# A decoder layer on one core: GpSimd overwrites the small router logits, and every engine's order is laid out anew

## The reference, cut to what matters

```python
x = _layernorm(x + _L0_attn_ref(x, ...))     # gated recurrence, 16-head attention, gated feed-forward
x = _layernorm(x + _L0_xattn_ref(x, ctx, ctx, mask, ...))   # attention over a context
x = _layernorm(x + _L0_ffn_ref(x, Wr, Wi, Wo))              # 8 experts, 2 chosen per token
```

```python
probs = jax.nn.softmax(xf @ Wr, axis=-1)      # 8 router logits per token
topk_p, topk_i = jax.lax.top_k(probs, 2)
# output: the sum over the two chosen experts of topk_p * (xf @ Wi[e] @ Wo[e])
```

## Time and profile before

| | us |
|---|---|
| median of 3 runs | 226.48 (226.40 to 226.54) |
| profiled execution | 226.43 |
| its span, first to last instruction | 224.5 |
| PE busy | 207.8 |
| DVE busy | 183.7 |
| ACT busy | 172.1 |
| POOL busy | 140.3 |

### The profile page before, as it was taken

The page is one execution under the profiler, slowest core; times in us unless marked ns, Lnnn a source line. Parts: engine busy times, 40 slices in busy tenths (PEclk is TensorE's granted clock), DMA queues, the critical chain, the costliest instruction groups (busy, mean ns, idle before and its releaser), DMA issues.

```text
span 224.5 us, 6962 instructions
## 1 busy us (share of the span) xinstructions
PE 207.8 (93%) x2170; PEld 173.5 (77%) x2170; DVE 183.7 (82%) x667; ACT 172.1 (77%) x663; POOL 140.3 (62%) x302
## 2 busy tenths in 40 slices
PE   7889999999999999999999999999989999998840
PEld 3568988999988799799778988798786899884310
DVE  3573775579879789988998999989988897999984
ACT  4799988987798796889699889986668867646730
POOL 5464535637568775777468766975648847547452
PEclk9999999999999999999999999999999999999997
DMA  4988745555742324002400555445460000000001
GB/s 99 252 256 191 181 110 134 149 149 137 172 107 52 105 55 108 0 7 49 108 1 4 123 140 127 109 116 102 127 154 13 5 25 15 16 0 1 12 23 35
DMA packets 33716, 20.05 MB, mean 89 GB/s; under 512 B 20497, under 2 KB 31249, under 8 KB 33681
## 3 DMA queue, kind: packets, MB, share of 16 engines
q1 hardware_dynamic: 32992, 19.35, 34.2%
q10 hardware_dynamic: 688, 0.26, 0.4%
HBM read 14.16 MB, written 5.24 MB: 86 GB/s over the span
## 4 chain that ended last, share of the span: by engine, by line
PE 49%; DVE 14%; DMA 9%; SPq 8%; issue 7%; ACT 7%; POOL 5%; POOLq 0%; DVEq 0%; ACTq 0%
PE ps L966 8%; DMA k_stack<-qk_scratch 5%; PE ps L931 5%; PE ps L843 4%; PE ps L1048 4%; SPq L276 4%; PE ps L898 4%; PE ps L920 4%; PE ps L989 4%; DMA ctx_sb<-in_ctx_dram 3%; PE ps L900 2%; PE ps L877 2%; PE ps L857 2%; DVE acc L2488 2%; ACT probs L1707 2%
## 5 line engine op out<-in xcount | busy, mean ns | idle before, releaser
L2373 DVE TENSOR_REDUCE neg_max<-ps 128x4 f32<-128x512 f32 x64 | 43.1, 677 | 4.7 <-PE ps L900 4.4
L1707 ACT ACTIVATE probs<-ps 128x512 f32<-128x512 f32 x64 | 38.4, 606 | 4.8 <-PE ps L920 4.5
L464 POOL TENSOR_TENSOR lrs<-mv,neghalf 128x1 f32<-128x1 f32 x48 | 26.5, 553 | 24.0 <-DVE mv L2418 8.4
L464 POOL TENSOR_TENSOR rs<-ss,neghalf 128x1 f32<-128x1 f32 x48 | 27.1, 567 | 20.7 <-ACT junk L1626 20.5
L966 PE MATMUL ps<-xT,guT 128*128 128x128 f32 x256 | 34.0, 276 | 0.0
L1048 PE MATMUL ps<-w_moe,y2T 128*128 128x512 f32 x64 | 32.6, 599 | 0.4 <-ACT terms L1786 0.4
L966 PEld LDWEIGHTS ps<-xT,guT 128*128 128x128 f32 x256 | 31.2, 192 | 0.3
L524 POOL TENSOR_SCALAR_AFFINE_SELECT probs<-probs 128x600 f32<-128x600 f32 x32 | 24.2, 758 | 8.1 <-ACT probs L1707 7.8
L898 PE MATMUL ps<-k_stack,q_stack 125*128 125x128 bf16 x256 | 24.9, 219 | 1.3 <-DMA k_stack<-qk_scratch 1.3
L920 PE MATMUL ps<-q_stack,k_stack 128*128 128x128 bf16 x256 | 24.8, 219 | 0.0
L920 PEld LDWEIGHTS ps<-q_stack,k_stack 128*128 128x128 bf16 x256 | 18.8, 99 | 3.8 <-issue 2.3
(11 more groups left out here) (156 smaller groups left out, 584.9 us busy)
## 6 DMA issues: line engine op xcount, KB each, us to landing
q_stack<-qk_scratch SPq DMA_DIRECT2D x48, 96.0 KB
k_stack<-qk_scratch SPq DMA_DIRECT2D x48, 96.0 KB
qk_scratch<-qk_parts SPq DMA_DIRECT2D x16, 192.0 KB, 2.2
ctx_sb<-in_ctx_dram SPq DMA_DIRECT2D x4, 256.0 KB, 3.5
qk_scratch<-qk_parts SPq DMA_DIRECT2D x16, 64.0 KB, 2.4
out_dram<-x_all SPq DMA_DIRECT2D x16, 64.0 KB, 1.6
x_all<-in_x_dram SPq DMA_DIRECT2D x2, 256.0 KB, 3.1
raw<-in_L_ffn_Wi_dram SPq DMA_DIRECT2D x1, 512.0 KB, 6.0
```

The lines of the kernel that those rows point to most:

```text
L464: nc.gpsimd.tensor_tensor(dst, src, neghalf[:], ALU.pow).then_inc(S[rsd], 1)
L1707: nc.scalar.activation(probs[:, b, n, :, :], view("probs", 4 * k + n), ACT.Exp, scale=HD ** -0.5).then_inc(S["att_p"], 1)
L2373: nc.vector.tensor_reduce(neg_max[:, b, QUARTER * n:QUARTER * n + QUARTER], view("scores", 4 * k + n), AX_X, ALU.max, negate=True).then_in ...
```

## The change: what it does

The overwriting of the six columns moves from DVE to POOL, as a step `moe_pad` of its own between `moe_top` and `moe_choose`; `moe_choose` waits for it:

```diff
+            def moe_pad(k):
+                b = k % 2
+                after(pool, "moe_top", k + 1)
+                nc.gpsimd.memset(top[:, b, CHOSEN:EXPERTS], NO_LOGIT).then_inc(S["moe_pad"], 1)
...
             def moe_choose(k):
                 b = k % 2
-                nc.vector.memset(top[:, b, CHOSEN:EXPERTS], NO_LOGIT).then_inc(S["moe_pick"], 1)
-                after(dve, "moe_pick", 3 * k + 1)
+                after(dve, "moe_pad", k + 1)
                 nc.vector.match_replace(moe_new[:, b, :], top[:, b, :], moe_lg[:, b, :], -NO_LOGIT).then_inc(S["moe_pick"], 1)
-                after(dve, "moe_pick", 3 * k + 2)
+                after(dve, "moe_pick", 2 * k + 1)
```

Waits that the new orders imply are left out, and waits that they need are put in:

```diff
-            def power(src, dst, ready, k, rsd, used):
+            def power(src, dst, ready, k, rsd):
-                after_all(pool, (ready, k + 1), (used, k - 1))
+                after(pool, ready, k + 1)
...
             def ffn_residual(k):
-                after(pool, "ffn_z", k - 1)
...
             def moe_add(k):
-                after(pool, "moe_high", k - 1)
...
             def att_values(k):
-                after(pe, "max_v", k + 1)
...
             def ffn_hidden(k, fill, g, done):
+                after(pe, "ffn_xT", k + 1)
...
             def gru_squares(k):
+                after_all(act, ("gru_rs", k - 1))
...
             def gru_tanh(k):
+                after(act, "gru_xs", k - 1)
+                after(act, "gru_decay", k - 1)
...
             def ctx_copy(k):
-                after(act, "ctx_kv_ps", k - 1)
```

More of the change, by code:

```diff
@@ L49 @@
[L49 to L62, removed]
@@ L372, in _ @@
             parts_stack(4)
+            parts_save(5)
             load_ctx(3)
-            parts_save(5)
             load_small()
@@ L377, in _ @@
             parts_stack(5)
+            parts_save(6)
             load_x(3)
-            parts_save(6)
             max_stack(4)
@@ L389, in _ @@
             max_stack(8)
+            store(0)
             parts_save(9)
             parts_stack(9)
+            store(1)
+            max_stack(9)
             parts_save(10)
-            max_stack(9)
             parts_stack(10)
-            store(0)
             parts_save(11)
-            store(1)
             store(2)
@@ L411, in _ @@
             parts_save(15)
-            store(5)
             max_stack(13)
@@ L416, in _ @@
             max_stack(15)
+            store(5)
             store(6)
@@ L757, in _ @@
             xat_ln_power(14)
+            moe_pad(13)
+            moe_pad(14)
             moe_ln_power(11)
@@ L762, in _ @@
             moe_ln_power(12)
+            moe_pad(15)
             moe_ln_power(13)
@@ L1324, in _ @@
             ffn_gate(6)
-            moe_experts(3, 0)
+            ffn_up(6)
             moe_logits(4)
@@ L2719, in _ @@
             moe_top(3)
[L2720 to L2741 removed]
+            moe_moments(2)
+            moe_choose(3)
+            moe_weights(3)
+            gru_scan(10)
+            ffn_silu(6)
+            ffn_product(6)
+            moe_layernorm(1)
+            xat_add_mask(5)
+            moe_top(4)
+            ffn_out(6)
+            moe_choose(4)
+            ffn_stats(6)
+            moe_weights(4)
+            ffn_moments(6)
+            moe_mix(3)
+            ffn_layernorm(6)
+            gru_out(10)
+            xat_reciprocal(5)
+            maxima(9, 0)
+            att_reciprocal(7)
+            gru_input(11)
             att_divide(7)
[L2743 removed]
             maxima(9, 1)
             moe_sum(3)
+            xat_out(5)
+            xat_stats(5)
+            gru_scan(11)
             xat_moments(5)
@@ L2757, in _ @@
             qk_rest_of(10)
+            moe_layernorm(2)
+            moe_top(5)
+            att_out(8)
             gru_input(12)
-            moe_top(5)
+            moe_sum(4)
+            moe_choose(5)
             gru_scan(12)
-            att_out(8)
+            moe_weights(5)
+            moe_stats(4)
+            ffn_silu(7)
             xat_reciprocal(6)
-            moe_moments(2)
+            moe_moments(3)
+            ffn_product(7)
             xat_out(6)
-            moe_choose(5)
-            moe_weights(5)
-            ffn_silu(7)
-            moe_layernorm(2)
-            ffn_product(7)
-            moe_sum(4)
-            moe_stats(4)
             gru_out(12)
             xat_stats(6)
+            moe_moments(4)
+            gru_input(13)
             xat_moments(6)
-            moe_moments(3)
             moe_mix(5)
@@ L2856, in _ @@
             maxima(13, 2)
-            moe_top(8)
             maxima(13, 3)
@@ L3016, in _ @@
             moe_layernorm(12)
+            moe_moments(13)
             moe_choose(15)
-            moe_moments(13)
             moe_weights(15)
```

1328 lines of the change are left out of this document (664 added, 664 removed).

## The result

The changed kernel takes 230.52 us (median of 4, 230.02 to 230.70), the kernel before 226.51 beside it: ratio 1.0173, 95% interval 1.0155 to 1.0192. It is 4.0 us slower where 0.6 us faster was forecast, and outside the range. In a second timing it took 228.46 (6 executions, 228.12 to 229.67) beside 226.64: 1.0094 (1.0058 to 1.0131). Executions over 1.5% above the fastest of the same kernel (one of b1, one of b4) are left out throughout.

A forecast was written before the change was run, and what follows sets the result against it. PE was taken to bound 40 to 200 us, DVE 200 to 214, then a chain of single steps. Terms -0.55, -0.20 and +0.18 sum to -0.57: 226.43 becomes 225.86, with 0.05 to the median 225.9 us; range 224.2 to 227.6.

The forecast's parts named there:

- The five overwritings: Term: DVE loses the overwritings of tiles 11 to 15, from 202.26 us on, at 0.11 us each: 0.55 us off.
- nothing that can be measured: Rival, chance 0.20 without the lock: DVE's saving ends in later waits after 214 us; 0.11 us off, 226.4 us.
- The rival of POOL's queue: Rival, chance 0.12: DVE waits for POOL's long steps at tiles 0, 3, 4, 10; 2.6 us, about half seen, 227.2 us.
- The lock: Rival, chance 0.06: DVE's layer norm holds POOL's overwriting for tiles 10 and 11; 0.3 us, giving 226.2 us.
- Waits left out and put in: Term: 96 powers, 16 residual sums and the adds lose a wait, ACT gains some; nothing, at most 0.3 us gained.
- keep_busy: Term: three single products leave PE's early waits; nothing, at most 1.1 us gained, and no loss of clock.
- The order of the end: Term: expert products fill PE's waits for ACT, 0.20 us off; moe_moments(12) ahead of tile 15's layer norm, 0.18 more.
- The order of the middle: Term: SP's transfers and some PE steps move; 0, bounds -0.9 and +1.0. As slower rival: 226.9 us, chance 0.14.

The follow-up runs named there:

- b1: Changed kernel with three head edits: two tile turnings in other PSUM banks, ACT's copy of tile 1 ahead of the squares of tile 2; 229.38 us, ratio 1.0170.
- b4: Changed kernel with the three head edits of b1 and nine more products of zeros in PE's tail waits; 230.08 us, ratio 1.0174.
- c1: Kernel before with only the overwriting given to POOL, placed where POOL is next free; 225.66 us, ratio 0.9975.
- h2: The changed kernel as it is, timed a second time; 228.46 us, ratio 1.0094.
- a2: Kernel before with only the overwriting given to POOL, at the changed kernel's neighbours in POOL's list; 230.20 us, ratio 1.0177.
- e1: Kernel before without its three single keep_busy products of zeros in the head; 226.72 us, ratio 1.0017.
- a1: Changed kernel with the overwriting put back on DVE; 231.74 us, ratio 1.0225.
- b3: Changed kernel with PE's order of the kernel before from the last ffn_down on; 230.62 us, ratio 1.0192.
- h1: Splice: steps and banks of the kernel before up to 36.8 us, then the changed kernel's, with seventeen products of zeros in the tail; 227.12 us, ratio 1.0034.
- g1: b4 with eight more products of zeros around tile 15's turning for the experts and its logits; 228.31 us, ratio 1.0110.
- b2: Kernel before with PE's order of the changed kernel from the last ffn_down on; 227.64 us, ratio 1.0060.
- d1: Splice: steps and banks of the kernel before up to the first scores (24.7 us), then the changed kernel's; 230.13 us, ratio 1.0159.

## Why the prediction was wrong, step by step

*The five overwritings, -0.55: the size came out, the place did not.* c1 does this alone and gains 0.25% (0.02 to 0.49%), 0.6 us. The trip is 0.20 us for 0.22, and hidden in the changed kernel. But the 0.55 us was to come behind 200 us (the first of the five stands at 200.31, not 202.26, and the rival's 0.86 us of free DVE are those of the window from 200), and no profile shows it there. From the last `ffn_down` to the end of the span before takes 24.0 us, c1 23.8, and h2, also without a fall ahead of PE's last products, 24.0. The other 1.0 us by which c1's profile is shorter is gained before 200 us, where the sum had nothing and single executions differ by as much. So the gain in the tail shows as 0.2 us, near the 0.11 of the rival "nothing that can be measured", and that c1's total met the forecast is luck as far as the profiles show.

*The rival of POOL's queue: right in kind, wrong in size.* It does not happen in the changed kernel. Where it does (a2) the four waits are 5.9 us where 2.6 was priced, one of them 2.55, and the kernel is 3.8 us slower: two thirds of the waits are seen, where the rival took half, since PE stood behind DVE.

*The lock (the rule of the Trainium skill, page "SBUF — State Buffer", section "Who interferes with whom").* No DVE wait for POOL's `top` shows in the changed kernel. Two of its 16 overwritings (at 190.48 and 219.94 us) meet the start of a layer norm, for 0.05 us, and neither is longer than usual (0.10 and 0.34 us). That is too short to tell, and no run took the lock by itself, so the rule is neither shown nor refuted.

*Waits left out and put in, 0.* No run separates them.

*keep_busy, 0 and no loss of clock: right as far as tried.* e1 has the clock at 1.00. But I looked for the clock in the wrong stage, by the busy share of one window. The order that came with the change emptied 12 to 13 us (1.31 us of wait), and a1 and b3 fell to 0.50 right there; the changed kernel's two profiles did not.

*The order of the end, -0.20 + 0.18: the step that failed most.* Without a clock fall these two terms come out as nothing, as their sum does: between the last `ffn_down` and the turning of tile 15 h2 takes 13.68 us and before 13.61, +0.07 for -0.02 (and for -0.35 with the three overwritings that lie in it). But the expert products that I moved into two waits were taken from later, and 206 to 210 us was left with 2.84 us of PE in 4. I priced the clock only for the three small products, and not for the moved ones. With the fall the same stretch takes 15.54 us: the term that I had as 0.20 gained measured 1.9 lost.

*The order of the middle, 0, bounds -0.9 and +1.0.* Inside the bounds: from the first scores to the last `ffn_down` the changed kernel loses 0.4 us (2.3 against 1.9), h2 0.2, less than single executions of one list differ there.

*What had no term at all: the banks and the order of the head.* "All of HOME is new" stands in the change, and the sum has no line for it. In before PE's longest wait for ACT between 6 and 25 us is 0.60 us; the new layout has one of 1.31. Measured +1.9 us at 25 us, in both profiled executions. With before's head in its place the changed kernel comes 1.3 us earlier at 200 us (h1 against h2, one execution each) and 1.7 us by the timed runs (h1 against g1). Which list or bank carries it is open: the three edits I picked from the waits gave 0.3 us back at 25 us and 0.2 to 0.4 at 200. PE's share of the loss is waits, not work, as its list has three products fewer.

The sum by spans: 224.5 + 2.1 by the last `ffn_down` + 0.1 in the tail = 226.7 without a fall (h2: 226.6), and 224.5 + 2.3 + 1.9 = 228.7 with one (228.6). As times these are 228.28 and 230.35 us; both lie over the range's upper end, 227.6, which took in a wait in the middle and one for POOL, but no head and no clock.

## What to carry to other kernels

When a change comes with lists and banks laid out anew, price the layout as a change of its own (here first of all the first 25 us), since lists and banks lean on one another: one kernel's order on the other's banks made waits that neither had (1.07 us in b2, 0.78 in d1). Moving PE's work forward into its waits can lose more than it gains if the place it came from runs thin; look at PE by short windows along the tail and ask what a clock of 0.5 would cost for what follows. An instruction of 0.1 us given to another engine costs what stands ahead of it in that engine's queue with its waits; placed where that queue is free it cost nothing (c1).

## What the runs showed that I had not expected

One program gave 230.0 to 230.7 us in one timing and 228.1 to 228.6 in four of six executions of another, with the same lists: the granted clock fell to 0.50 at 210 us in the one profile and not in the other, after the same 1.2 of 2 us. The Trainium skill (page "TensorE: Matmul & The Clock Gate", section "Part 1: The HAM clock gate (the "warmup" mystery)") says that the watch on PE's activity runs freely and is not started anew with the kernel. The traces agree so far as the clock fell behind this thin stretch in one execution and not in another. The kernel before never showed it in its profile before PE's end: its thinnest 2 us ahead of its last products are 1.13 (212 to 214 us), and its 24 timed executions beside a1 to b4 lie between 225.10 and 226.80 us, while b1 and b4, say, spread over 3.1 and 3.2 us. Later timings of it spread more: the 17 beside h1 and h2 lie between 225.62 and 228.80, the slowest at a mean clock of 0.984.

Work that nobody reads may have made a kernel faster: g1 is b1 with seventeen products of zeros more, and its ratio to before is 1.0110 (1.0089 to 1.0132) where b1's is 1.0170 (1.0126 to 1.0213). The chips differ, the intervals touch, and the changed kernel moved by more between two timings, so that it is not shown; no cost of the seventeen shows either.
